# A graph layer on one core: edge loads ahead of x, fills between row writes, first norm's rows on ScalarE, two accumulators in DRAM instead of three

## The reference

```python
xn = _layernorm(x)                                       # rows of 256, no gain, no bias
gathered = edge_weight[:, None] * xn[dst]                # 100,000 rows
new_x = jax.ops.segment_sum(gathered, src, 6250)         # the graph branch: a scatter-add
out1 = new_x @ hamilton1                                 # 256x256
out1 = tanh((out1 - mean0) * rsqrt(var0 + eps) * gamma + beta)    # mean over all nodes
gnn = out1 @ hamilton2
# mix: q, k, v of xn; layer norms of k and v; kv = k^T v over all nodes; a two-layer head
x = x + gnn + mix(xn)
x = x + ffn(_layernorm(x))                               # 8 experts, top 2, hidden 1024
```

## Time and profile before

| | us |
|---|---|
| median of 3 runs | 2349.8 |
| the profiled execution, its own time | 2357.27 |
| its span, from the first to the last instruction | 2355.6 |
| first put | 109.07 |
| last put | 1349.22 |
| PE, DVE, ACT, POOL busy | 1902.5, 1675.5, 1123.4, 1281.4 |

### The profile page before, as it was taken

One profiled execution on the slowest core, in us unless ns is written; L12 is line 12 of the kernel. 1 busy time (PEld: TensorE's weight loads), 2 busy tenths in 40 slices (PEclk: granted clock), 3 DMA queues, 4 the chain that ended last, 5 costly groups with the idle time before them and its releaser, 6 DMA issues. The chain is left out here.

```text
span 2355.6 us, 37938 instructions
## 1 busy us (share of the span) xinstructions
PE 1902.5 (81%) x11157; PEld 1580.3 (67%) x11157; DVE 1675.5 (71%) x5298; ACT 1123.4 (48%) x2232; POOL 1281.4 (54%) x811
## 2 busy tenths in 40 slices
PE   2469998687887878886887456875899999999995
PEld 1447776565665556655766323761899999999995
DVE  4848898687866867674333156668888888888884
ACT  1324443222233232323222113436899999999993
POOL 1447787577777888776777700000355544455542
PEclk8679998799998999998999679775999999999997
DMA  7878877477787787868888764232688888888886
GB/s 227 279 204 154 170 115 124 74 127 118 128 143 143 127 165 131 179 104 170 182 180 175 92 203 136 79 121 99 187 232 231 231 234 235 234 232 231 231 233 169
DMA packets 325850, 401.91 MB, mean 171 GB/s; under 512 B 34983, under 2 KB 267196, under 8 KB 325506
## 3 DMA queue, kind: packets, MB, share of 16 engines
q1 hardware_dynamic: 193964, 256.71, 35.2%
q0 software_dynamic: 103008, 103.83, 32.5%
q10 hardware_dynamic: 28662, 38.84, 5.4%
HBM read 251.13 MB, written 154.55 MB: 172 GB/s over the span
## 5 line engine op out<-in xcount | busy, mean ns | idle before, releaser
L1094 POOL DMA_INDIRECT acc_dram<-third x566 | 917.9, 1622 | 336.0 <-issue 141.4
L2010 POOL DMA_INDIRECT sum_dram<-node,small x112 | 194.7, 1738 | 315.9 <-DVE node L1939 298.8
L1880 PE MATMUL bank<-down_parts 128*128 128x256 f32 x2688 | 335.4, 284 | 0.0
L1867 PE MATMUL bank<-up_parts 128*128 128x256 f32 x2688 | 333.1, 284 | 2.3 <-DVE up_parts L1897 2.3
L1867 PEld LDWEIGHTS bank<-up_parts 128*128 128x128 f32 x2688 | 327.9, 193 | 2.7 <-DVE up_parts L1897 2.7
L1880 PEld LDWEIGHTS bank<-down_parts 128*128 128x128 f32 x2688 | 325.3, 191 | 0.0
L551 PE MATMUL bank<-work,third 128*128 128x256 f32 x1132 | 296.3, 404 | 27.9 <-ACT third L1049 26.5
L1049 ACT ACTIVATE third<-bank 128x512 f32<-128x512 f32 x283 | 168.7, 597 | 289.3 <-DMA acc_dram<-third 226.8
L857 DVE TENSOR_SCALAR third<-fixed,third 128x128 f32<-128x128 f32 x566 | 165.5, 374 | 157.2 <-PE bank L540 135.6
L551 PEld LDWEIGHTS bank<-work,third 128*128 128x128 f32 x1132 | 219.1, 206 | 64.7 <-ACT third L1049 33.3
L1992 POOL DMA_INDIRECT node<-xh_dram,small x112 | 138.2, 1234 | 220.1 <-DVE small L1693 186.3
(11 more groups left out here) (265 smaller groups left out, 3119.3 us busy)
## 6 DMA issues: line engine op xcount, KB each, us to landing
turned<-in_w_up SPq DMA_DIRECT2D x56, 1024.0 KB
turned<-in_w_down SPq DMA_DIRECT2D x56, 1024.0 KB
work<-src_dram SPq DMA_DIRECT2D x141, 256.0 KB
acc_dram<-fixed SPq DMA_DIRECT2D x15, 1280.0 KB, 11.1
work<-xn_dram SPq DMA_DIRECT2D x146, 128.0 KB
work<-acc_dram SPq DMA_DIRECT2D x72, 256.0 KB, 3.5
at_dram<-turned ACTq DMA_DIRECT2D x48, 256.0 KB
work<-at_dram ACTq DMA_DIRECT2D x24, 512.0 KB
```

The lines of the kernel that those rows point to most:

```text
L1094: e.indirect_dma_start(acc_dram[i], bass.IndirectOffsetOnAxis(put_i[:, t:t + 1], 0), M[:, t % (2 * QUAD), :], None, compute_op=ALU.add).th ...
L1867: k = e.matmul(ps, W1s[:, 2 * b + wp, q, h * P:(h + 1) * P], xTs[:, 2 * b + xp, q, :], start=(q == 0 and (wp, xp) == TERMS[0]), stop=(q == ...
L1880: k = e.matmul(bank[5 + c][:, 0:D], hTs[:, hp, h, c * P:(c + 1) * P], W2s[:, 2 * b + wp, h, :], start=(h == 0 and hp == 0 and wp == 0), st ...
L2010: e.indirect_dma_start(sum_dram, bass.IndirectOffsetOnAxis(slot_i[:, n:n + 1], 0), yb[:, i % 2, c, :], None, compute_op=ALU.add).then_inc( ...
```

## The change

Four edits, all in the parts described above.

- **Edge loads.** The full rows of `src` and of the weights go out first on ScalarE's queue, those of `dst` and both pieces of `dst` in rows of 512 first on SP's, ahead of x. The tails of the rows follow on ScalarE's queue. The memsets that they wait for come first on VectorE. `src_dram` is written by ScalarE's queue, ahead of the weights.
- **Fills.** Three fills stand ahead of the first spreads, then come the first four spreads, and then each of the seven row writes is followed by one fill. With two accumulators these ten are all.
- **First norm.** VectorE makes the root's input, the reciprocal and `shift = -mean * rstd`; the rows are made by ScalarE as `Identity(rstd * x + shift)`, and its copies of transposed rows follow two rows behind.
- **Accumulators.** `N_ACC` is 2 and `EARLY` is (0,), so the puts go to two accumulators in turn from the first. The node stage loads two and adds once.

```diff
-N_ACC = 3
+N_ACC = 2
-EARLY = (4, 12)
+EARLY = (0,)
...
+        small.again()
+        small(10 * NT)
+        shift = small(NT)
...
         def vector_edges(e):
+            for ap, v in ((raw_dst, N - 1), (raw_src, NP_ - 1), (raw_w, 0.0)):
+                e.memset(ap[:, full, :], v).then_inc(s_set, 1)
+            e.memset(raw_dstq[:, 1, :], N - 1).then_inc(s_set, 1)
+            e.memset(zeros, 0.0).then_inc(s_set, 1)
             e.memset(ones[:, :], 1.0).then_inc(s_set, 1)
-            e.memset(zeros, 0.0).then_inc(s_set, 1)
...
-                    vec.done(e.bn_aggr(mv[:, t, :], stats[:, t, :]))
-                vec.wait()
-                e.tensor_scalar(ve[:, a:b], mv[:, a:b, 1], EPS, None, ALU.add).then_inc(s_ve, 1)
+                    k = e.bn_aggr(mv[:, t, :], stats[:, t, :])
+                k.then_inc(s_ve, 1)
                 e.wait_ge(s_root, c + 1)
-                e.reciprocal(rstd[:, a:b], ve[:, a:b]).then_inc(s_rstd, 1)
-                e.wait_ge(s_rstd, c + 1)
-                if c >= 2:
-                    e.wait_ge(s_xnd[c % 2], 16 * (c // 2))
-                    e.wait_ge(s_xnTp, CT * (c - 1))
-                    e.wait_ge(s_xplus, c - 1)
-                for t in range(a, b):
-                    e.tensor_scalar(xn_ring[:, c % 2, t - a, :], X[:, t, :], mv[:, t, 0:1], rstd[:, t:t + 1],
-                                    ALU.subtract, ALU.mult).then_inc(s_xn, 1)
+                vec.done(e.reciprocal(rstd[:, a:b], ve[:, a:b]))
+                e.wait_ge(s_ve, c + 1)
+                vec.wait()
+                e.scalar_tensor_tensor(out=shift[:, a:b], in0=mv[:, a:b, 0], scalar=-1.0, in1=rstd[:, a:b],
+                                       op0=ALU.mult, op1=ALU.mult).then_inc(s_rstd, 1)
...
         def scalar_edges(e):
+            edge_rows(e, raw_src, src)
+            edge_rows(e, raw_w, ew)
             e.wait_ge(s_set, SET_QUADS)
+            for ap, dram in ((raw_src, src), (raw_w, ew), (raw_dst, dst)):
+                last_edges(e, ap, dram)
...
+            e.wait_ge(s_split, 1)
+            e.dma_start(src_dram.rearrange("(g t) j -> t g j", t=P), src_f).then_inc(s_srcd, 16)
...
+            norm_root(0)
             for c in range(G):
                 a, b = c * CT, (c + 1) * CT
+                e.wait_ge(s_rstd, c + 1)
+                if c >= 2:
+                    e.wait_ge(s_xnd[c % 2], 16 * (c // 2))
+                    e.wait_ge(s_xplus, c - 1)
                 for t in range(a, b):
+                    if c >= 2:
+                        e.wait_ge(s_xnTp, t - 2 * CT + 1)
+                    e.activation(xn_ring[:, c % 2, t - a, :], X[:, t, :], ACT.Identity, bias=shift[:, t:t + 1],
+                                 scale=rstd[:, t:t + 1]).then_inc(s_xn, 1)
+                    if t - a == 5 and c + 1 < G:
+                        norm_root(c + 1)
+                    if t >= 2:
+                        turned_row(t - 2)
...
         def sync_edges(e):
+            edge_rows(e, raw_dst, dst)
+            e.dma_start(raw_dstq[:, 0, :], dst[0:P * QE].rearrange("(q j) -> q j", j=QE)).then_inc(s_edges, 16)
+            e.wait_ge(s_set, SET_QUADS)
+            e.dma_start(raw_dstq[0:q_full - P, 1, :], dst[P * QE:q_full * QE].rearrange("(q j) -> q j", j=QE)).then_inc(s_edges, 16)
...
-            for c in range(G):
-                a, b = c * CT, (c + 1) * CT
-                if c < 5:
-                    fill(c)
-                e.wait_ge(s_xn, b)
-                e.dma_start(xn_dram[a * P:b * P, :].rearrange("(t p) d -> p t d", p=P), xn_ring[:, c % 2]).then_inc(s_xnd[c % 2], 16)
+            for n in range(3):
+                fill(n)
...
+            for c in range(G):
+                a, b = c * CT, (c + 1) * CT
+                e.wait_ge(s_xn, b)
+                e.dma_start(xn_dram[a * P:b * P, :].rearrange("(t p) d -> p t d", p=P), xn_ring[:, c % 2]).then_inc(s_xnd[c % 2], 16)
+                fill(3 + c)
...
-            for n in range(5, 5 * N_ACC):
+            for n in range(3 + G, 5 * N_ACC):
                 fill(n)
...
-                e.tensor_tensor(sums[:, 0, 0:n * D], sums[:, 0, 0:n * D], sums[:, 2, 0:n * D], ALU.add).then_inc(s_accs, 1)
-                e.wait_ge(s_accs, 2 * u + 1)
                 e.tensor_tensor(sums[:, 0, 0:n * D], sums[:, 0, 0:n * D], sums[:, 1, 0:n * D], ALU.add).then_inc(s_accs, 1)
```

More of the change, by code:

```diff
@@ L270, in gps_layer @@
         EDGES, WEIGHTS = 16 * 12, 16 * 7
-        SET_ONES, SET_ZEROS, SET_EPS, SET_X, SET_EDGES, SET_QUADS, SET_BIAS = 1, 2, 4, 5, 8, 9, 11
+        SET_QUADS, SET_ZEROS, SET_ONES, SET_EPS, SET_X, SET_BIAS = 4, 5, 6, 8, 9, 11
         def x_landed(c):
@@ L775, in vector_edges @@
             e.memset(X[:, NT - 1, :], 0.0).then_inc(s_set, 1)
-            for ap, v in ((raw_src, NP_ - 1), (raw_dst, N - 1), (raw_w, 0.0)):
-                e.memset(ap[:, full, :], v).then_inc(s_set, 1)
-            e.memset(raw_dstq[:, 1, :], N - 1).then_inc(s_set, 1)
             e.memset(bkv, 0.0).then_inc(s_set, 1)
@@ L1002, in product_scalar, with edge_rows, last_edges @@
                 yield
-        def scalar_edges(e):
[L1005 to L1011, removed]
+        def edge_rows(e, ap, dram):
+            e.dma_start(ap[:, 0:full, :], dram[0:e_full].rearrange("(g t j) -> t g j", t=P, j=P)).then_inc(s_edges, 16)
+        def last_edges(e, ap, dram):
+            e.dma_start(ap[0:last_rows, full, :],
+                        dram[e_full:e_full + last_rows * P].rearrange("(t j) -> t j", j=P)).then_inc(s_edges, 16)
+            e.dma_start(ap[last_rows:last_rows + 1, full, 0:E_TAIL],
+                        dram[E - E_TAIL:E].rearrange("(t j) -> t j", t=1)).then_inc(s_edges, 16)
+        def scalar_edges(e):
+            edge_rows(e, raw_src, src)
+            edge_rows(e, raw_w, ew)
             e.wait_ge(s_set, SET_QUADS)
-            e.dma_start(raw_dstq[:, 0, :], dst[0:P * QE].rearrange("(q j) -> q j", j=QE)).then_inc(s_edges, 16)
-            e.dma_start(raw_dstq[0:q_full - P, 1, :], dst[P * QE:q_full * QE].rearrange("(q j) -> q j", j=QE)).then_inc(s_edges, 16)
+            for ap, dram in ((raw_src, src), (raw_w, ew), (raw_dst, dst)):
+                last_edges(e, ap, dram)
             e.dma_start(raw_dstq[q_full - P:q_full - P + 1, 1, 0:E - q_full * QE],
                         dst[q_full * QE:E].rearrange("(q j) -> q j", q=1)).then_inc(s_edges, 16)
+            e.wait_ge(s_split, 1)
+            e.dma_start(src_dram.rearrange("(g t) j -> t g j", t=P), src_f).then_inc(s_srcd, 16)
             e.dma_start(Wqkv, w_qkv.rearrange("(k p) n -> p k n", p=P)).then_inc(s_w, 16)
@@ L1024, in scalar_edges, with norm_root, turned_row @@
             e.dma_start(cols[:, 0:4, :].rearrange("p a b -> p (a b)"), cols_mix).then_inc(s_w, 16)
+            def norm_root(c):
+                a, b = c * CT, (c + 1) * CT
+                e.wait_ge(s_ve, c + 1)
+                e.activation(ve[:, a:b], mv[:, a:b, 1], ACT.Sqrt, bias=eps_col).then_inc(s_root, 1)
+            def turned_row(t):
+                e.wait_ge(s_xnTp, t + 1)
+                e.activation(xnT[:, :, t * P:(t + 1) * P], bank[4 + t % 4][:, 0:2 * P].rearrange("p (k n) -> p k n", k=KC),
+                             ACT.Copy).then_inc(s_xnT, 1)
+            e.wait_ge(s_set, SET_EPS)
+            norm_root(0)
             for c in range(G):
                 a, b = c * CT, (c + 1) * CT
-                e.wait_ge(s_ve, c + 1)
-                e.activation(ve[:, a:b], ve[:, a:b], ACT.Sqrt).then_inc(s_root, 1)
+                e.wait_ge(s_rstd, c + 1)
+                if c >= 2:
+                    e.wait_ge(s_xnd[c % 2], 16 * (c // 2))
+                    e.wait_ge(s_xplus, c - 1)
                 for t in range(a, b):
-                    e.wait_ge(s_xnTp, t + 1)
-                    e.activation(xnT[:, :, t * P:(t + 1) * P], bank[4 + t % 4][:, 0:2 * P].rearrange("p (k n) -> p k n", k=KC),
-                                 ACT.Copy).then_inc(s_xnT, 1)
+                    if c >= 2:
[6 more added lines that the diff above has]
+                        turned_row(t - 2)
+            turned_row(NT - 2)
+            turned_row(NT - 1)
             def between(q):
@@ L1404, in tensor_nodes @@
             for u in range(pairs):
-                e.wait_ge(s_accs, 2 * u + 2)
+                e.wait_ge(s_accs, u + 1)
                 for t in in_pair(u):
```

4 lines of the change are left out of this document (1 added, 3 removed).

## The result

The changed kernel takes 2574.5 us (median of four runs, 2564.3 to 2582.6), the kernel before 2352.5 with a fourth run of it. The ratio is 1.093, with a 95% interval of 1.085 to 1.100. The forecast was 2549 us, in a range of 2430 to 2640, and "slower". The profiled execution took 2567.4 us with a span of 2566.0.

The account below looks back on a forecast made before the run. The pitch of GpSimd's puts was taken as the bound. Last put at 98 + 565 x 2.58 = 1555.7 us, 206.5 later, with -7 for the nodes gives +199.5 on 2357.3: 2556.8 profiled, 2549 us as median, range 2430 to 2640.

Parts of the forecast that it names:

- The bound: GpSimd's puts: their pitch, 2.141 us before the change, sets what the stage costs and counts 565 times.
- The pitch: Time per put on two accumulators, (1.56 + T) / 2: 2.58 us forecast, between 2.40 and 2.85.
- T: End of a put's instruction to the next start on its accumulator: 3.6 us taken, mean bounded by 3.24 and 4.14.
- The 90 waits and 91.4 us: Puts held by a landing with three accumulators, of 566; taken to have a mean T of 4.74 us.
- The estimate from the skill: Put of 128 KB estimated at 2.3 us, pitch 1.93 us on two accumulators; the prediction held the trace against it.
- The start: Prologue: first put at 98 us instead of 109.07, put 17 at 139; whole start gains 35 us.
- The limit by bytes: Prologue: 29.1 MB at 302 to 351 GB/s take 83 to 96 us; first window issued at about 88.
- Nodes: Node stage: one add of 0.60 us less in each of twelve chunks, -7 us; nothing for fewer loads.
- A: Rival: T falls to its floor of 2.95 us, pitch 2.26 us, 2368 us in all; chance 0.08.
- B: Rival: not slower, the landing wait is hidden, pitch stays 2.141 us, 2301 us; chance 0.04.
- C: Rival: TensorE's clock falls to 0.65 and it becomes the bound, pitch 2.76 us, 2651 us; chance 0.08.
- The signs: Pairs of 4.9 to 5.4 us, some 400 of 566 released by landings, first put 94 to 107, last 1450 to 1640.

Follow-up runs that it names:

- fills_after_writes: Changed kernel with three accumulators, the third's fills one per quad, and the three fills ahead of the first spreads moved behind the last three row writes: 2341.7 us, 0.992.
- edges_behind_x: Changed kernel with three accumulators, the third's fills one per quad, and the loads of dst behind x again on SP's queue: 2352.5 us, 0.994.
- rows_on_vector: Changed kernel with three accumulators, the third's fills one per quad, and the rows of the first norm back on VectorE: 2327.3 us, 0.982.
- two_in_before: Kernel before with two accumulators alone, one add in the node stage, prologue's edits left out: 2616.2 us, 1.105 of the kernel before.
- one_accumulator: Changed kernel with one accumulator, so every put waits for the landing of the one before it: 3746.9 us in one run.

## Why the prediction was right, step by step

**The bound.** That the pitch of the puts sets the stage was shown by both halves: the same 2.62 to 2.63 us with two accumulators under either prologue, and 2.14 to 2.15 us with three. The wait for the landing was the right mechanism.

**The pitch.** 2.58 us was forecast and (1578.48 - 95.55) / 565 = 2.625 us came. This is the term that was off: T = 3.6 us was a choice between 3.24 and 4.14, and 3.64 came. T was short by 0.04 us, which is 0.02 in the pitch; the other 0.025 are the mean duration of a put, 1.61 us, where I used the least, 1.56. Over 565 puts the 0.045 us make +25 us. The first put (-2.5) and the nodes (-12 beyond mine) take off 14.5, which leaves some 2556.8 + 11 = 2568 us, within 1 us of the profiled execution (2567.4). The median is 7 us above that execution, whereas I had taken 7.5 off for the kernel before; that is the rest of the 25 us between 2549 and 2574. My reason for taking T below the middle (two puts in one burst share the delay) was not tested.

That 3.64 fell between my bounds of 3.24 and 4.14 was in part luck, because their inputs were not what I took them for. The 90 waits and 91.4 us of the earlier trace rows are not all of puts on three accumulators: 5 waits with 19.7 us belong to the first sixteen puts, which ran on one or two. And the count leaves out what the releaser hides: another 75 waits with 100.1 us are put down to ScalarE's copy, part of which are the same kind of wait. The first error makes the mean of a held put too long, the second makes the held puts too few.

**The estimate from the skill.** By "DMA: Bandwidth & Descriptors" of the Trainium skill, section "Anatomy of one DMA — SWDGE (gpsimd) path", two accumulators would have cost nothing, with an estimate of 2.3 us for a put. The least T measured with a put alone in flight is 2.78 us and the mean 3.11, so the measurement decides against the estimate, as the earlier trace rows had. From the end of its instruction a put lands after 2.2 to 2.3 us, which is what the estimate gives for the whole DMA; what it leaves out of T is the 0.7 us from the landing to the next start.

**The start.** The first put was forecast at 98 us and came at 95.55, the seventeenth at 139 and came at 137.84. (My range for it should have begun at 93 us, 83 + 10.1, and not at 94.) The limit by bytes, argued then, has the DMA engines at 0.99 busy and 337 GB/s up to the first window behind it, and `fills_after_writes`; `edges_behind_x` shows where it ends, since late tables leave those engines idle. The edges landed for use at 14.2 us where I had said 12. The step that was only half right is ScalarE's: a row costs 0.5 us and not 0.42, a copy's share of a chunk is less, and a chunk took 5.6 us instead of 6.1; `rows_on_vector` shows that neither matters. The stop of 8.8 us for the ring buffer was not in my working. It cost nothing that shows: without it `fills_after_writes` was no sooner.

**Nodes.** -7 us were forecast and -18.9 came from the last put to the end. Of this 13.8 us lie between the last put and the first tanh (114.7 and 100.9 us), and `two_in_before` has 101.1 us there, so they belong to the accumulator. The chain of a chunk lost 0.73 us, twelve chunks make 8.8 us, and the rest is probably the ramp, where the first sum can start a third of the loads sooner: the loads which I had given nothing. No run tries that by itself. The other 5 us are between tanh and the first gather of the experts (185.1 us before, 179.7 now). Four more kernels with the same code there took 179.6 to 193.2 us, so I do not count them as an effect of the change.

**The rivals.** A (T at its floor) would have needed 2.95 us; one put alone in flight comes to 3.11, two to 3.64. It was right in kind: T is shorter with fewer puts in flight and thinner traffic, and my own expectation of `one_accumulator` was met only at its lower edge. B (hidden) fell: the wait stands on the pitch in full. C (TensorE the bound) fell too: its granted clock in the stage is 0.86 (0.92 before), between its levels of 1.2 and 2.4 GHz and nearer the upper, and it is busy 1040 of 1441 us, so it has time to spare. With one accumulator the clock fell to 0.70 and TensorE was still idle half of the time (busy 1242 of 2578 us), so the clock went down with the slower puts and did not cause them.

**The signs.** Most were as said. One was not: landings as releasers are 215 of the 566, not 400. Counted by idle time, 395 puts waited, most of them for a landing under one of the two names.

## What to carry to other kernels

When an operation must wait for the landing of an earlier one on the same target, its cost is (instruction + T) / n for n targets, as long as that is more than the engine's own step. T runs from the end of one instruction to the start of the next on the same target, and is more than the latency of the transfer alone; look in the trace for a stretch that already runs with fewer targets. Take n so that the cost falls below the engine's own step. Here two targets cost 2.62 us against a step of 1.86; for three the formula gives (1.61 + 3.64) / 3 = 1.75 us, an estimate from the T of two. The measured 2.15 us with three are more, because 116 of the 549 puts still stood longer than 0.35 us, and a fourth target costs as much as it brings. When all DMA engines are full in a prologue, count the bytes ahead of the first use. Here moving the rows of the norm between engines brought nothing, and loading the edges sooner did.

## What the runs showed of the hardware

The granted clock of TensorE was 0.54 from 25 to 50 us of the changed kernel, where TensorE worked 9.3 of 25 us, and 0.50, that is 1.2 GHz, from 50 to 95.55 us, where it worked 31.4 of 45.6 us. It had been 1.00 in the first 25 us, where it worked 5.3 us. The rows of the first 50 us of that stretch, with PE, PEld, DVE, ACT, POOL, PEclk, DMA share and GB/s:

```profile
25.00:50.00 25.00, 9.25 (x28) 4.06 (x28) 16.14 (x67) 12.16 (x30) 7.96 (x2) 0.54 0.96 328
50.00:75.00 25.00, 18.56 (x54) 7.83 (x54) 10.08 (x51) 21.85 (x59) 11.97 (x3) 0.50 1.05 380
```

The same rows show the DMA engines full over 50 us, at 328 and 380 GB/s.

VectorE was held up by GpSimd. Four `tensor_scalar` operations that took 1.11 us elsewhere took 4.78 us while GpSimd added its rows:

```profile
75.52 4.78 DVE L856 TENSOR_SCALAR third<-fixed,third 128x128 f32<-128x128 f32 x4
...
88.07 1.11 DVE L856 TENSOR_SCALAR third<-fixed,third 128x128 f32<-128x128 f32 x4
```

```profile
75.33 4.12 POOL L1110 TENSOR_TENSOR node<-node,work 128x1792 f32<-128x1792 f32 x1 [1.59 <-ACT work L1052]
```

GpSimd's operation ends at 79.45 us, and VectorE's four are done 0.85 us later, so the first of them stood until then. The next addition does the same: it ends at 85.58 us, and four `tensor_scalar` that began at 81.67 us end at 86.43, again 0.85 us later. The `bn_stats` that ran beside the earlier additions kept their 2.38 us. The page "SBUF — State Buffer" of the Trainium skill describes this in the section "SBUF: two separate sides" as a lock, held for a whole instruction, on a pair of ports that VectorE and GpSimd share. The rows agree.
